# A graph and expert kernel on one core: 84 constant matmuls placed in two waits of TensorE

## The reference

```
h  = layernorm(x)
deg, agg = segment_sum(1, dst), segment_sum(h[src], dst)
h  = h @ W_self + b_self + (agg / max(deg, 1)) @ W_neigh
h  = layernorm(h) * gamma + beta;  h = where(h >= 0, h, alpha * h)
x  = x + h + layernorm(x)                       # graph layer
t  = layernorm(x)
top_vals, top_idx = top_k(t @ gate.T, 2);  routing_w = softmax(top_vals)
h  = silu(einsum('td,efd->tef', t, w1))         # only of chosen experts
h_mean = mean of h over the tokens of each expert
y_mean = einsum('ef,edf->ed', h_mean, w2)
x  = x + sum_k routing_w[k] * y_mean[top_idx[k]]
```

## Time and profile before

| | us |
|---|---|
| median of three runs | 1616.33 |
| lowest, highest | 1616.28, 1617.91 |
| profiled execution, own time | 1613.05 |
| its span, first to last instruction | 1610.9 |
| busy: PE, DVE, ACT, POOL | 1167.9, 1078.0, 894.4, 984.4 |
| mean granted TensorE clock | 0.895 |

### The profile page before, as it was taken

The page is one execution under the profiler, slowest core; times in us unless marked ns, Lnnn a source line. Parts: engine busy times, 40 slices in busy tenths (PEclk is TensorE's granted clock), DMA queues, the critical chain, the costliest instruction groups (busy, mean ns, idle before and its releaser), DMA issues.

```text
span 1610.9 us, 36408 instructions
## 1 busy us (share of the span) xinstructions
PE 1167.9 (72%) x7640; PEld 629.2 (39%) x7648; DVE 1078.0 (67%) x2594; ACT 894.4 (56%) x1939; POOL 984.4 (61%) x1254
## 2 busy tenths in 40 slices
PE   4989899999666555655556565676666339999975
PEld 2545444444322222222222222234444226676741
DVE  6776326666677576777878777656657975777626
ACT  3455455555645444444445544437666787788810
POOL 6223177676777777777777777777777006766400
PEclk9999999999979788889978878879999759999975
DMA  6445278877888888888888889888888527777548
GB/s 208 144 146 170 84 229 276 266 232 253 271 277 276 269 253 248 258 290 293 303 294 298 297 270 302 253 242 252 251 248 243 212 87 234 244 234 238 145 168 299
DMA packets 140572, 384.92 MB, mean 239 GB/s; under 512 B 22286, under 2 KB 22416, under 8 KB 140452
## 3 DMA queue, kind: packets, MB, share of 16 engines
q0 software_dynamic: 76416, 250.05, 51.6%
q1 hardware_dynamic: 63508, 132.49, 22.9%
q10 hardware_dynamic: 528, 1.05, 0.2%
HBM read 323.78 MB, written 59.72 MB: 238 GB/s over the span
## 4 chain that ended last, share of the span: by engine, by line
PE 42%; POOL 22%; issue 16%; DMA 9%; DVE 4%; ACT 3%; POOLq 2%; DVEq 0%; SPq 0%; ACTq 0%
POOL work L642 22%; PE ps L912 14%; PE ps L1013 12%; DMA work<-table,work 7%; PE ps L1106 6%; PE ps L1117 3%; PE ps L1108 3%; POOLq L637 2%; ACT slots L827 1%; ACT wparts L817 1%; DMA work<-in_x 1%; PE ps L958 1%; PE ps L1179 1%; PE ps L1153 1%; DVE slots L1650 1%
## 5 line engine op out<-in xcount | busy, mean ns | idle before, releaser
L642 POOL DMA_INDIRECT work<-table,work x832 | 792.6, 953 | 290.6 <-issue 235.3
L1013 PE MATMUL ps<-work 128*128 x2056 | 560.8, 423 | 329.2 <-DMA work<-table,work 314.2
L1013 PEld LDWEIGHTS ps<-work 128*128 128x128 f16 x2056 | 213.7, 104 | 566.4 <-issue 416.6
L770 ACT ACTIVATE work<-work,ones 128x512 f16<-128x512 f16 x259 | 185.4, 716 | 300.4 <-PE ps L1016 300.0
L764 ACT ACTIVATE work<-iota_row,work 128x128 f16<-128x128 f32 x1040 | 331.3, 390 | 31.6 <-ACT work L770 23.9
L912 PE MATMUL ps<-wparts,slots 128*128 128x512 f16 x1176 | 273.0, 383 | 17.9 <-DVE slots L1300 11.8
L701 POOL DMA_INDIRECT slots<-x_d,betab x114 | 110.0, 965 | 139.5 <-DVE betab L1580 70.9
L912 PEld LDWEIGHTS ps<-wparts,slots 128*128 128x128 f16 x1176 | 112.1, 99 | 140.1 <-DVE slots L1300 14.3
L1382 DVE TENSOR_SCALAR inv<-ps 128x1 f32 (+2 forms) x49 | 7.8, 158 | 233.3 <-PE ps L1016 227.5
L1106 PE MATMUL ps<-work,wparts 128*128 x456 | 155.3, 381 | 0.9 <-ACT wparts L856 0.3
L856 ACT COPY wparts<-ps 128x1024 f16<-128x1024 f16 x114 | 115.2, 1011 | 38.6 <-PE ps L1117 37.4
(11 more groups left out here) (281 smaller groups left out, 1536.5 us busy)
## 6 DMA issues: line engine op xcount, KB each, us to landing
work<-in_x SPq DMA_DIRECT2D x96, 256.0 KB, 2.9
work<-in_w_t SPq DMA_DIRECT2D x48, 512.0 KB, 4.2
work<-table,work POOLq DMA_INDIRECT x832
table<-work SPq DMA_DIRECT2D x48, 256.0 KB, 2.0
x_d<-work SPq DMA_DIRECT2D x48, 256.0 KB
x_d<-slots SPq DMA_DIRECT2D x48, 256.0 KB
slots<-x_d SPq DMA_DIRECT2D x48, 256.0 KB
out_x<-slots SPq DMA_DIRECT2D x48, 256.0 KB
```

The costliest lines, as they stand in the source:

```text
L642: pool.indirect_dma_start(out=gath[:, g % GRING, w, :], out_offset=None, in_=table[:, :], in_offset=bass.IndirectOffsetOnAxis(ap=idx_all[: ...
L770: act.activation(hot[:, slot, :, :], away[:, slot % 2, :, :], ACT.Relu, bias=ones[:, 0:1], scale=-1.0).then_inc(c_hot, 1)
L1013: pe.matmul(ps[:, ds(bank, 1), :], hot[:, s, w, :], gath_row[:, ds(at + (2 * w + half) * D, D)].unsqueeze(1), start=False, stop=True, skip ...
```

## The change

A helper `keep_busy(n)` is added to TensorE's program. It issues n matmuls of a constant: the f32 identity matrix read as f16, 128 columns of it stationary and 256 moving, written to the first 256 columns of PSUM bank 5. Nothing reads the result, no semaphore is waited for or raised. It is called in four places: 8 matmuls behind the transpose in the first `powers` and 6 behind its spreading matmul (34 with the next), 20 ahead of `project(0)`, and 50 between the last matmul of the expert lists and the waits in front of the first `turn`.

```diff
+            filler = ident[:, :].bitcast(f16)
+
+            def keep_busy(n):
+                for _ in range(n):
+                    pe.matmul(ps[:, 5, 0:2 * P], filler[:, 0:P], filler[:, 0:2 * P], start=True, stop=True)
+
             def powers(n, cols, bank, turns):
 
                 most(n, cols, bank, turns)
+                if turns == 1:
+                    keep_busy(8)
                 spread(n, bank, turns)
+                if turns == 1:
+                    keep_busy(6)
...
             for i in range(TILES):
                 if i + 1 < TILES:
                     turn_x(i + 1)
+                if i == 0:
+                    keep_busy(20)
                 project(i)
...
             last.then_inc(i_map, 1)
+            keep_busy(50)
             pe.wait_ge(v_w1, 16 * EXPERTS)
             pe.wait_ge(e_done, 1)
```

## The result

The changed kernel takes 1619.53 us (median of 14 runs, 1617.35 to 1622.55), the kernel before 1616.13 us (14 runs, 1614.13 to 1620.64): a ratio of 1.0019, 95% interval 1.0011 to 1.0028. By this ratio it is 3.1 us slower, where 4 us faster was forecast. The profiled execution took 1619.03 us with a span of 1616.8 us.

A forecast was written before the change was run, and what follows sets the result against it. POOL's issue was taken to bound the gather stage, TensorE the expert stage. Gains of 1.7 and 1.5 us, taken as 2.0 us each for the median, gave 1616.33 - 4.0 = 1612.3 us, range 1609.5 to 1616.5.

The forecast's parts named there:

- So I cost the fillers at nothing: Ahead of `project(0)`: the 20 fillers fit in a 2.73 us wait, 2.14 us at the upper clock level.
- The slower one: Rival 4: fillers don't raise the clock, stay at 0.213 us and delay both places; 1620.9 us; 5%.
- First gain: `project(0)` takes 2.76 instead of 4.45 us; 1.70 us carried through POOL's earlier gathers to the end of their stage.
- slacks of 0.28 and 0.06 us: Margins by which `project(3)` and ACT L719 at 42.14, moved 1.70 us earlier, would still follow work that does not move.
- Rival 1: The first gain is absorbed, by used-up slacks or a gather stage that gives nothing: 1614.3 us; 15%.
- Second gain: Start of the experts: faster turns and first `hidden` bring `turn(2)` 1.5 us earlier, carried through 114 slots.
- `hidden(0)` starts there: Start of the experts: `hidden(0)` starts when `turn(1)` frees the array, at 1329.66 instead of 1330.41, 0.75 us earlier.
- So I take the clock to stay up: After the 50 fillers: idle of up to 1.5 us and some 0.8 us between turns does not drop the clock.
- Rival 2: The clock falls between the fillers' end and `hidden(0)`; second place gives nothing or 0.4 us: 1614.0 us; 10%.
- The rule on transposes: The Trainium skill says transposes don't engage the fast clock, so `turn_x` adds nothing before the first projection; trace speaks rather against.
- Rival 3: Eight transposes break the run-up, the 20 fillers run slow and end 1.5 us late: 1614.1 us; 7%.
- The correction for the median: The runs' median lies 3.3 us above the profiled execution, so each place was taken at 2.0 us, 4.0 us together.

The follow-up runs named there:

- e4: The whole change plus 44 one-column matmuls in the wait for `e_reach`, against the kernel before: 0.9984, measured again 0.9985.
- f1: The whole change plus 4 one-column matmuls in the wait for `e_reach`, against the kernel before: 0.9996.
- f2: The whole change plus 16 one-column matmuls in the wait for `e_reach`; only profiled, once: edge slot 1.81 us.
- e2: The kernel before with only the 50 matmuls ahead of the experts, the other three calls left out: 1.0000 of before.
- f3: The whole change plus 24 one-column matmuls in the wait for `e_reach`; only profiled, once: edge slot 1.81 us.
- g1: The change with 58 fillers instead of 50, 6 between the first two turns, 4 behind the second, and 26 one-column matmuls: 0.9991 of before.
- e1: The kernel before with only the 34 matmuls ahead of the first projection, `keep_busy(50)` left out: 1.0001 of before.

## Why the prediction was wrong

**What bounds the kernel.** Right as far as it went: both places run at the lower level, and the expert stage is TensorE's. What it left out is that this stage is a loop with an edge; before, the edge slot is only 0.04 us longer than the others, so it did not show.

**"So I cost the fillers at nothing."** This is the step that failed, and not by the fillers' own time. As work they do cost nothing, as said: the 20 end at 20.4 and the 50 at 1327.8, in their waits. As instructions they moved the loop to a place where the jump back costs 0.27 us more on average, 17 times: 4.6 us. The slots between give 0.6 back (1.754 us on average instead of 1.761), most of it in two slots that take 2.03 and 2.19 us before and 1.75 after, so that 4.0 us stay, as much as all that was to be gained. Of my rivals none was this. The slower one, fillers that stay at 0.213 us, did not occur: the 20 took 2.35 us.

**First gain, 1.7 us, with slacks of 0.28 and 0.06 us.** The term itself is right, 4.45 to 2.76 us. The first projection takes 2.76 us in all nine profiles with the 34 fillers, and 4.24 to 5.30 us (4.87 on average) in the ten without. What came through to the first gather is less. With the fillers it starts at 196.88 us on average, without at 198.19: 1.3 us. And that it lasts from there isn't shown: the first expert turn comes at 1329.6 and at 1330.0 us on average, 0.4 us apart, where single profiles of one group lie over 3 us apart. The two slacks that I named held (`project(3)` starts at 33.66, 33.67 was forecast), and a third thing that doesn't move was missing. SP loads a tile of `x` for DVE's statistics when ACT L719 of tile 5 is done, and this ACT instruction is behind the one that waits for POOL. So the load keeps its time, while DVE comes for the tile earlier and has to wait for it (all engines, after):

```profile
33.15 0.43 SPq L393 DMA_DIRECT2D work<-in_x  x1
...
37.25 0.69 DVE L1298 BATCH_NORM_STATS2 stats<-work 128x6 f32<-128x512 f32 x1 [0.91 <-DMA work<-in_x]
...
41.12 1.25 PE L922 MATMUL ps<-wparts,slots 128*128 128x512 f16 x5 [1.25 <-DVE slots L1313]
```

and in e4, where the same load lands in time:

```profile
33.20 0.44 SPq L393 DMA_DIRECT2D work<-in_x  x1
...
36.31 0.68 DVE L1303 BATCH_NORM_STATS2 stats<-work 128x6 f32<-128x512 f32 x1
...
40.47 1.90 PE L926 MATMUL ps<-wparts,slots 128*128 128x512 f16 x8 [0.53 <-DVE slots L1318]
```

The load was issued at the same time in both and before; DVE now comes for it at 36.3. Where it lands in time the projection of tile 5 starts at 40.47, 1.6 us earlier than before, otherwise at 41.12, 1.0 us earlier. Of the nine profiles four have this wait (first gather 196.9 to 198.5, mean 197.9), five don't (195.4 to 197.2, mean 196.1). The split fits the wait, but that the wait alone makes it was not tried; more waits for loads of `x` come later in both groups. Rival 1 was half right: the gain was partly absorbed, but by a load.

**Second gain, 1.5 us.** Two steps of it failed. That `turn(1)` frees the array at 1329.66 and "`hidden(0)` starts there": it starts 1.18 us or more after `turn(1)` has begun, with fast turns or slow, so the 0.75 us of an earlier start don't exist. What is left is the faster `hidden`, and from the first turn to the third the five profiles with the 50 fillers in which the clock held (e4 twice, f1 twice, f2) give 3.84 us on average against 4.78 over the ten without the 50: 0.9 us. "So I take the clock to stay up": it did in these five and fell in three, after, e2 and f3 (4.97 us, worse than without fillers by 0.2). The gaps were as long as forecast, 1.46 and 0.73 us in after and 1.10 and 0.69 in e4, but there was a third, 0.57 us ahead of `hidden(0)`, and I had compared them one by one with gaps of the gather stage, where there is more work between them; that this is why it fell was not tried. Rival 2, at 10%, was underrated: three of eight. On average the second place is worth 0.5 us.

**The rule on transposes.** Rival 3, that the eight transposes break the run-up and the 20 fillers start slow, fell: in after they take 2.35 us, and over all nine profiles 2.35 to 2.73. In after the eight transposes in front of them already take 1.60 us against 1.97 us before, so the pace rose while TensorE was at them. The Trainium skill's sentence (TensorE: Matmul & The Clock Gate, Part 4: PE-mode transpose) that the fast clock doesn't engage for them is not what this trace shows. Whether they count as work no run tells, since 14 fillers stand ahead of them.

**The sum,** with what was measured: 1.3 us at the first gather, if it lasts, and 0.5 us make 1.8 us gained on average, and 4.0 us are lost in the loop, so it should be 2.2 us slower. Measured: 3.1 us slower with the slow edge (1.8 to 4.5 by the interval). With a fast edge the change is 2.6 and 2.4 us faster in e4, 1.5 us with g1's added fillers, and nearly nothing, 0.6 us, in f1, whose interval reaches from 2.6 us faster to 1.3 us slower. On average that is 1.8 us. Against it stand e1 and e2, each with one place alone: both measured nothing, by intervals that reach 1.3 and 1.5 us to the faster side. So a gain is shown for the whole change, about half of the 4.0 us forecast, but not how it divides between the places; that it comes by the clock is read from the profiles.

The correction for the median, which took 2.0 us for each place instead of 1.7 and 1.5, rests on the thought that executions on average start worse than the profiled one. For the first projection that is so: 4.87 us on average without fillers, so 2.1 us to gain instead of 1.7, but this didn't come through to the first gather. At the expert start the ten profiles without the 50 fillers lose 0.2 us more than the first, not 0.5. The lower end of the forecast gain, 1.4 and 1.5 us, is 2.9 us and not 2.8.

## What to carry to other kernels

Instructions that cost no time where they stand can cost it where they push the others: when a change adds or removes instructions ahead of a hot loop, compare the loop's edge with its inside, slot by slot, before explaining the time by what the change does. A control that only shifts the code (here matmuls of one element, 28 ns each, in a wait) tells placement from effect in one run, and here 4 of them removed the loss. And a gain in front of a chain is worth what its unmoved neighbours allow: list the transfers among them too, and look at what stands between the end of a wait and the work that is to start earlier.

## What the runs showed of the hardware

A TensorE loop of 263 instructions that jumps back 17 times takes 0.25 to 0.27 us more on average at each jump back if its first instruction stands at 211 or 212 of 256, in a program of 11178 to 11602 instructions. At 208 it takes some 0.2 us more at every second jump. At 4, 44, 84, 112, 144, 148, 216, 220 and 244 it does not, and 256 instructions further it does again. These are measurements of one loop in one program.

After a long wait, the first `hidden` behind the entry of the loop starts 1.18 us after the matmuls in front of it have started (up to 1.34 us in seven of nineteen profiles), with these matmuls at either clock level.
